# A store of one combination moved behind the return of the probabilities, on one DMA queue

## The reference

```python
x_n   = rmsnorm(layernorm(x)) * ln_weight
h_q, h_k, h_v = x_n @ w_q.T, ctx @ w_k.T, ctx @ w_v.T      # 32 heads of 128
score = einsum('bqhd,bkhd->bhqk', h_q, h_k) + position_bias  # masked, softmax over k
attn  = einsum('bhqk,bkhd->bqhd', softmax(score), h_v)
x     = x + tanh(g_xattn[0]) * (layernorm(x) + attn @ w_out.T)
```

## Time and profile before

| | |
|---|---|
| time, median of 3 runs | 943.73 us (943.26 to 944.18) |
| profiled execution, its own time | 943.65 us |
| its span in the trace | 941.9 us |
| TensorE matmul busy | 934.0 us (99%) |
| VectorE, GpSimd, ScalarE busy | 595.1, 497.0, 403.9 us |
| mean rate of the DMA engines | 215 GB/s |

### The profile page before, as it was taken

One profiled execution on the slowest core, in us unless ns is written; L12 is line 12 of the kernel. 1 busy time (PEld: TensorE's weight loads), 2 busy tenths in 40 slices (PEclk: granted clock), 3 DMA queues, 4 the chain that ended last, 5 costly groups with the idle time before them and its releaser, 6 DMA issues.

```text
span 941.9 us, 15363 instructions
## 1 busy us (share of the span) xinstructions
PE 934.0 (99%) x4818; PEld 791.2 (84%) x4818; DVE 595.1 (63%) x1021; ACT 403.9 (43%) x1088; POOL 497.0 (53%) x463
## 2 busy tenths in 40 slices
PE   8999999999999999999999999999999999999998
PEld 7888788888888888888888888888888888888885
DVE  4788945385538554854476547664576967766654
ACT  5765524352434333423333334433442336658730
POOL 3847574555346453646374636563556326688640
PEclk9999999999999999999999999999999999999999
DMA  8136587775677576767678666867686656223002
GB/s 288 46 126 233 194 290 268 265 264 203 259 259 269 218 267 246 275 248 267 223 268 278 245 245 233 291 244 255 236 278 255 242 205 208 121 97 105 1 1 90
DMA packets 71268, 202.60 MB, mean 215 GB/s; under 512 B 10176, under 2 KB 25024, under 8 KB 70208
## 3 DMA queue, kind: packets, MB, share of 16 engines
q1 hardware_dynamic: 70224, 200.83, 59.4%
q10 hardware_dynamic: 1008, 1.32, 0.4%
HBM read 175.90 MB, written 26.21 MB: 215 GB/s over the span
## 4 chain that ended last, share of the span: by engine, by line
PE 93%; DVE 2%; DMA 2%; ACT 1%; POOL 1%; SPq 0%; issue 0%; DVEq 0%; ACTq 0%
PE bank L1982 27%; PE bank L1998 18%; PE bank L2059 17%; PE bank L2164 11%; PE bank L2031 6%; PE bank L2015 6%; PE bank L1958 3%; PE bank L2188 1%; PE bank L2245 1%; PE bank L2043 1%; PE bank L2309 1%; PE bank L2266 1%; DMA craw<-in_ctx 1%; DVE work_raw L1508 1%; POOL wvo L644 0%; DMA stage<-in_w 0%
## 5 line engine op out<-in xcount | busy, mean ns | idle before, releaser
L2059 PE MATMUL bank<-wvo,ao 128*128 128x512 f32 x768 | 179.7, 391 | 0.0
L1998 PE MATMUL bank<-wvo,ct 128*128 128x512 f32 x768 | 177.7, 390 | 0.0
L1998 PEld LDWEIGHTS bank<-wvo,ct 128*128 128x128 f32 x768 | 143.5, 188 | 29.3
L2059 PEld LDWEIGHTS bank<-wvo,ao 128*128 128x128 f32 x768 | 143.0, 188 | 29.3 <-issue 0.2
L644 POOL TENSOR_TENSOR wvo<-stage,wvo 128x512 fp32r<-128x512 f32 x64 | 85.5, 1358 | 143.2 <-ACT wvo L947 143.2
L1982 PE MATMUL bank<-ring,wkq 128*128 128x512 f32 x648 | 158.2, 391 | 0.0
L1982 PEld LDWEIGHTS bank<-ring,wkq 128*128 128x128 f32 x648 | 120.8, 188 | 24.9
L1469 DVE SCALAR_TENSOR_TENSOR acc<-bank,gated_rows,acc 128x512 f32<-128x512 f32 x128 | 93.1, 742 | 39.1 <-PE bank L2059 38.1
L993 ACT ACTIVATE bank<-bank,nmax 128x128 f32<-128x128 f32 x256 | 88.2, 351 | 62.6 <-DVE nmax L1431 62.6
L1460 DVE TENSOR_TENSOR ao<-bank,ao 128x512 fp32r<-128x512 f32 x64 | 44.0, 691 | 99.1 <-ACT ao L999 99.1
L1491 DVE TENSOR_TENSOR qt<-bank,qt 128x512 f32<-128x512 f32 x98 | 66.4, 690 | 57.0 <-PE bank L1982 55.5
(11 more groups left out here) (189 smaller groups left out, 1507.6 us busy)
## 6 DMA issues: line engine op xcount, KB each, us to landing
ring<-combined SPq DMA_DIRECT2D x214, 512.0 KB, 6.4
stage<-in_w SPq DMA_DIRECT2D x63, 512.0 KB, 4.4
passing<-turned_blocks SPq DMA_DIRECT2D x24, 512.0 KB, 2.9
keyed<-passing SPq DMA_DIRECT2D x96, 128.0 KB, 3.0
combined<-work SPq DMA_DIRECT2D x14, 512.0 KB, 3.6
xraw<-in_x SPq DMA_DIRECT2D x2, 1024.0 KB, 11.5
bias<-in_bias SPq DMA_DIRECT2D x8, 256.0 KB, 5.0
cs<-in_ctx SPq DMA_DIRECT2D x1, 2048.0 KB, 7.5
```

Source lines behind the costliest of these rows:

```text
L1998: mm = pe.matmul(bank[un_of[m][u] % RING][:, :], ct[:, i, c, b * P:(b + 1) * P], wvo[:, j, c, :], start=(c == 0 and i + j == 0), stop=(c = ...
L2059: mm = pe.matmul(bank[to][:, :], ao[:, h, p, b * P:(b + 1) * P], wvo[:, j, 2 * pair + h, :], start=(h == 0 and p + j == 0), stop=(h == 1 a ...
```

## The change

Within SyncE's list for group 0, the store of x's second combination goes behind the store and the return of head 2's probabilities. Nothing is added or removed, and no other engine's list changes.

```diff
@@ -489,9 +489,9 @@
                 sp.wait_ge(s_plain_lo, 8)
                 load(1, "k0", 0)
                 put(1, 0, 2)
-                put(1, 1, 3)
                 passed(0, 2)
                 back(0, "first", 2)
+                put(1, 1, 3)
                 sp.wait_ge(s_vo_lo, 8)
                 load(1, "q0", 1)
                 sp.wait_ge(s_plain_lo, 10)
```

## The result

The changed kernel takes 942.35 us, median of 22 runs (941.7 to 942.95), against 943.66 of the kernel before in the same sessions: a ratio of 0.9986, 95% interval 0.998 to 0.9991. That is 1.3 us less, a little more than the 0.9 that was forecast, and within the range. The profiled execution took 942.72 us.

What follows compares the result with a forecast made beforehand. TensorE, busy 934.0 of 941.9 us, bounds the kernel, so only its gaps can be won. Terms: -1.1 for the store, 0 for the return, +0.2 for the ports, together -0.9, giving 942.8 us; range 942.1 to 944.1.

Steps and rivals of the forecast that it cites:

- the whole gap goes: Rival at head 2's attention: store arrives after 2.6, ports cost nothing, 1.3 to 1.6 us gained, 942.2 to 942.4; chance 0.12.
- The place and its cause: Before head 2's attention in group 0: TensorE's 1.6 us gap comes from the put's 1 MB under way ahead of the probabilities.
- The term of the store: Store of head 2's probabilities: without the put ahead, arrival takes 2.8 us in place of 3.93, a gain of 1.1.
- The fetch: Return of head 2's probabilities: last fetch, 3.06 us before, has no cost from the put behind it, 0.2 as bound.
- v0: Load behind the put: arrives at 113.0, ScalarE waits nearly 2 us; up to 113.3 costs TensorE nothing at head 3's attention.
- The put's own arrival: The put's second half arrives at 110.4; ScalarE's overwrite of its source waits some 0.4 us, GpSimd starts at about 111.6.
- The ports: VectorE's steps 8 and 9 beside GpSimd: step 8 comes second, costing 0 to 0.45 us before project 8, 0.2 taken.
- Slower by v0: Rival at head 3's attention: late v0 holds ScalarE and then TensorE, a loss once past 114.4, up to 944.6; chance 0.11.
- nothing comes of it: Rival: the fetch loses what the store wins, taking 4.2, or a second wait eats the gain; 943.3 to 943.8, chance 0.22.

Runs made afterwards that it cites:

- e1: Changed kernel with the first of the put's two DMAs (512 KB) left ahead of the probabilities' store, the second behind the return: 942.36 us.
- e2: Kernel before with the put moved between the store of the probabilities and their return: 943.76 us.
- e3: Kernel before with one more store of 512 KB between the put and the store of the probabilities: 945.22 us.
- e5: Changed kernel with one more store of 512 KB behind the put, ahead of the loads: 942.97 us.
- e6: Changed kernel with two more stores, 1 MB, behind the put, ahead of the loads: 944.51 us, ratio 1.0011 to the kernel before.
- e0_again: The changed kernel once more, with no edit: 942.37 us.
- e4: Changed kernel with the load of v0 issued ahead of the load of q0: 942.03 us.
- e7: Changed kernel with the put moved on, behind the loads of q0 and v0 and of the bias: 944.73 us, ratio 1.0016 to the kernel before.

## Why the prediction was right

**The number.** The sum was -0.9 and -1.3 was measured. The median, 942.35, is inside the range but outside the forecast's own 942.5 to 943.1. It lies in the times of the rival "the whole gap goes" (942.2 to 942.4), which had 0.12 of the chance. What that rival named is what happened, a store of 2.6 and ports that cost nothing, though 0.2 us of the gap stayed. That the profiled execution took 942.72, almost the 942.75 of the forecast, is luck: it had lost 0.45 us in the last group.

**The place and its cause.** Right. The only gap of TensorE after the start-up was the return of head 2's probabilities, and 1.36 of its 1.56 us came from 1 MB standing ahead of them. e1, e2 and e3 show the line from three sides: 0, 1 and 1.5 MB ahead of the store give gaps of 0.2, 1.6 and 2.9 us, half a MB that is through in time gives 0.25, and 1 MB between store and fetches gives 1.7.

**The term of the store.** Predicted 1.1, measured 1.33. I took the arrival of a group 1 store, 2.8, as the time without the put; it is 2.60 in every kernel of this study that has the line free at this place. The nearer row was the put's own first half, 2.6, which I had kept as a bound.

**The fetch.** Predicted unchanged behind puts, and 3.06 was measured again.

**v0.** Predicted to arrive at 113.0, with 113.3 as the limit; measured 113.1, and the limit, from e5 and e6, is 113.3 to 113.4 (107.06 + 6.25 to 6.30). Counted from the attention of head 2 I had allowed only 5.9 us (113.3 less 107.4), so the limit is 0.35 wider than reckoned. The load was issued at 106.29, where 106.1 was reckoned, and needed 6.8 us. The way of reckoning was right, but that 113.1 meets 113.0 is partly luck. With the store's true 1.33 the same sum puts v0 at 112.8 against an attention at 107.2, 5.6 us after it, and that is e0_again's 5.64. In the first profile v0 was 0.5 later than that, which stays unexplained.

**The put's own arrival.** Predicted 110.4, measured 109.6 (4.7 us from its issue at 104.90), so ScalarE hardly waited for it, and GpSimd started at 110.85 and not at 111.6.

**The ports.** The other term that was off in size. The order did turn round, as foreseen: step 8 took 2.70. It ended at 114.31 and not at 115.3, since GpSimd had started 0.75 earlier. I took 0.2 us as the loss at `project` 8 and it was nothing. Step 9 ended at 116.56 of the 116.5 to 117.8 that I allowed, and `ao_lo(0, 3)` started at 118.65, 0.69 a half, for 119.97: 0.6 us of cover were left. e4 shows that even with GpSimd's subtractions close behind, VectorE doesn't end later. With 2.6 for the store and nothing for the ports, the sum would have been -1.3.

**The rivals.** Slower by v0 is a real mechanism; it decides in e6, with 1 MB more. That nothing comes of it didn't happen: the fetch took 3.06, not 4.2.

## What to carry to other kernels

A transfer that nobody waits for soon should not be issued closely ahead of one that stands on the chain. What the urgent one pays for are the bytes still in the line when its own data come: here 1 MB cost 1.33 us, and 512 KB issued 1.27 us ahead cost nothing. When it is moved back, price everything in the new order by the end of the whole train, and find who is last there: one position too early (between store and fetch) or one group of loads too late (behind v0), and the gain is gone or turned into a loss. The same gap can be closed by moving work of the waiting engine in front of it, and then the second remedy is worth nothing more.

## What the hardware showed that was not expected

Most issues on SyncE's queue take 0.32 to 0.43 us here, but some took 0.87 and 1.19 us (105.38 and 106.29 in the changed kernel, with 1.5 and 2 MB of earlier transfers not yet arrived); in e6 three in a row took 0.86, 1.19 and 1.20. So a queue with much under way can also hold the issuing engine, and with it everything behind. The bytes alone don't set it: in e3 an issue took 0.79 behind 1 MB (99.45), and in e7 one took 0.43 behind 1.75 MB (105.85). What does is open.

A gap of 2.91 us on TensorE brought its granted clock down to 0.50 in e3, for the first 6 us of work behind it, which cost about 3 us more than the gap. Behind the gaps of 1.92 and 2.02 us in the profiles of e7 and e6 it stayed up:

```profile
117.00:120.00 3.00, 2.55 (x19) 2.46 (x20) 0.16 (x1) 3.00 (x6) 3.00 (x3) 1.00 0.45 183
```

That is e7 right behind its gap, with the clock at 1.00. But a profile is one execution. The mean clocks of all timed executions say that it isn't always so. A mean of 0.998 or less stands at 5 of 11 executions of e7, 1 of 10 of e6, 1 of 11 of e2 (gap 1.70), 4 of 11 of e3 and 4 of 88 of the kernel before (gap 1.56; those beside the experiments), and at none of the 90 of the kernels with gaps of 0.73 or less. These executions took some 1 to 4 us longer than the median of the others of their kernel. Where in them the clock fell is not on record; that it was at the long gap is the reading that fits the counts. So the long gaps of this study probably cost more than their own length in some executions and not in others. A single profile doesn't show that.
